# A two-layer graph network on one core: the weight 1 of each node's edge to itself added by GpSimd to the landed stripes, not by a product in every octet of the edge stage

## What is computed

```python
def _gcn_conv(x, W, b, src, dst, ew, n_nodes):
    loop = jnp.arange(n_nodes)
    src2 = concatenate([src, loop]); dst2 = concatenate([dst, loop])
    ew2 = concatenate([ew, jnp.ones((n_nodes,))])
    deg = segment_sum(ew2, dst2)
    dinv = where(deg > 0, rsqrt(maximum(deg, 1e-30)), 0.0)
    norm = dinv[src2] * ew2 * dinv[dst2]
    return segment_sum((x @ W)[src2] * norm[:, None], dst2) + b
```

## Time and profile before

| | us |
|---|---|
| median of 3 runs | 2230.41 |
| lowest and highest | 2229.63, 2230.86 |
| span of the profiled execution (first to last instruction) | 2231.0 |
| busy in the span: PE | 2089.4 (94%) |
| DVE | 1653.8 (74%) |
| ACT | 1233.5 (55%) |
| POOL | 566.9 (25%) |

### The profile page before, as it was taken

The page is one execution under the profiler, slowest core; times in us unless marked ns, Lnnn a source line. Parts: engine busy times, 40 slices in busy tenths (PEclk is TensorE's granted clock), DMA queues, the critical chain, the costliest instruction groups (busy, mean ns, idle before and its releaser), DMA issues. The chain is left out here.

```text
span 2231.0 us, 47270 instructions
## 1 busy us (share of the span) xinstructions
PE 2089.4 (94%) x18287; PEld 1958.7 (88%) x18287; DVE 1653.8 (74%) x3108; ACT 1233.5 (55%) x2876; POOL 566.9 (25%) x406
## 2 busy tenths in 40 slices
PE   5659999999879999998999999999999999999997
PEld 3549999999779999997788999999988999999996
DVE  6899888886578888884667666565667768888885
ACT  5656555555537677674543444444444336767664
POOL 3100000000036777761000000000000015777775
PEclk9879999999989999998999999999999999999998
DMA  4424343333448778775003666466641026777776
GB/s 123 145 65 115 96 114 90 99 111 104 161 158 234 236 218 241 227 222 144 1 26 89 189 188 182 122 182 195 189 145 47 25 93 184 239 231 222 240 215 171
DMA packets 241114, 339.04 MB, mean 152 GB/s; under 512 B 33407, under 2 KB 202546, under 8 KB 240754
## 3 DMA queue, kind: packets, MB, share of 16 engines
q1 hardware_dynamic: 208908, 296.19, 42.4%
q0 software_dynamic: 28528, 35.76, 8.6%
q10 hardware_dynamic: 3446, 3.97, 0.6%
HBM read 258.89 MB, written 76.95 MB: 151 GB/s over the span
## 5 line engine op out<-in xcount | busy, mean ns | idle before, releaser
L2011 POOL DMA_INDIRECT SC<-xd,slot_i x128 | 181.6, 1419 | 1423.8 <-DVE slot_q L1647 1291.6
L2436 PE MATMUL bank<-WB_r,XN_r 128*128 128x448 f32 x1400 | 398.7, 366 | 0.4 <-DVE X L2253 0.4
L2390 DVE TENSOR_TENSOR WB_r<-WB,WB_r 128x448 fp32r<-128x448 f32 x350 | 214.8, 624 | 169.1 <-ACT WB_r L2385 169.0
L2385 ACT CAST WB_r<-WB 128x448 fp32r<-128x448 f32 x350 | 198.2, 568 | 244.8 <-PE bank L2436 242.9
L2436 PEld LDWEIGHTS bank<-WB_r,XN_r 128*128 128x128 f32 x1400 | 262.4, 188 | 23.0 <-DVE X L2253 0.8
L1941 PE MATMUL bank<-SC_r,WB_r 128*128 128x256 f32 (+1 forms) x2064 | 250.8, 280 | 8.4 <-issue 6.3
L1941 PEld LDWEIGHTS bank<-SC_r,WB_r 128*128 128x128 f32 x2064 | 244.3, 188 | 12.6 <-issue 12.4
L1061 ACT CAST WB_r<-bank 128x200 fp32r<-128x200 f32 x391 | 145.3, 372 | 164.7 <-PE bank L1045 163.9
L1956 PE MATMUL bank<-R_r,H_r 128*128 128x256 f32 x1752 | 216.6, 283 | 5.0 <-DVE R_r L1852 5.0
L1956 PEld LDWEIGHTS bank<-R_r,H_r 128*128 128x128 f32 x1752 | 210.4, 190 | 5.4 <-issue 5.4
L1804 ACT ACTIVATE wb_<-bank,WB 128x256 f32<-128x256 f32 (+1 forms) x344 | 133.3, 477 | 79.7 <-PE bank L1941 40.6
(11 more groups left out here) (462 smaller groups left out, 5139.1 us busy)
## 6 DMA issues: line engine op xcount, KB each, us to landing
WB<-adjw SPq DMA_DIRECT2D x350, 224.0 KB, 2.8
WB<-in_f_pack SPq DMA_DIRECT2D x127, 512.0 KB
WB<-in_f_pack SPq DMA_DIRECT2D x62, 640.0 KB
adjw<-X SPq DMA_DIRECT2D x24, 1600.0 KB, 7.6
WB<-in_f_pack SPq DMA_DIRECT2D x65, 516.0 KB
xd<-XN SPq DMA_DIRECT2D x15, 640.0 KB, 5.5
y<-X SPq DMA_DIRECT2D x10, 640.0 KB, 3.3
X<-y SPq DMA_DIRECT2D x6, 640.0 KB, 7.0
```

The costliest lines, as they stand in the source:

```text
L2011: e.indirect_dma_start(yin[i % 2][:, q * D:(q + 1) * D], None, XD, bass.IndirectOffsetOnAxis(ap=slot_i[:, 2 * i + q:2 * i + q + 1], axis=0 ...
L2385: e.copy(split_w(m)[0], RAW[m % PR]).then_inc(S("whigh"), 1)
L2390: e.tensor_tensor(al, RAW[m % PR], ah.bitcast(F32), ALU.subtract).then_inc(S("wlow"), 1)
L2436: mm_ = e.matmul(conv_bank(k, band, c)[:, 0:PW], x[st][:, o], y, start=(st == 0 and i == 0), stop=(st == T - 1 and i == 2))
```

## The change

The product of the identity is gone from every octet; the last of an octet's other products now ends the group and releases ACT. The bf16 copy of the identity goes with it. Instead `own_edges_pool` on GpSimd adds the identity (fp32) to the part of a landed stripe where src is dst, in both convolutions. Such a part is in the stripes that the diagonal crosses: four in each band, 28 in a convolution, 56 in all, of 128 x 128 or 128 x 64 numbers. ACT's rounding of these stripes waits for the addition (semaphore `own`). To have a semaphore for that, three others were merged into two that were there; who waits for whom in them stays as it was.

```diff
-    ident16, iota16 = r1_all[:, 1700:1764].bitcast(BF16), r1_all[:, 1764:1828].bitcast(BF16)
+    iota16 = r1_all[:, 1764:1828].bitcast(BF16)
...
-        c.add(e.tensor_copy(ident16, ident))
...
-        e.tensor_copy(beg4i, beg4).then_inc(S("begins"), 1)
+        e.tensor_copy(beg4i, beg4).then_inc(S("rows"), 1)
...
-        e.wait_ge(S("begins"), 1)
+        e.wait_ge(S("rows"), 2)
...
                 for p in (2, 3):
-                    e.matmul(bk[:, o + KEYS:o + 2 * KEYS], lo, key[:, p * KEYS:(p + 1) * KEYS],
-                             start=False, stop=False, skip_group_check=True)
-            weights = bk[:, 0:8 * KEYS].rearrange("p (q two n) -> p q two n", q=4, two=2)[:, :, 1, 2 * b:2 * b + 2]
-            e.matmul(weights, ident16, ident16[:, 8 * (w % 16):8 * (w % 16) + 8].rearrange("p (q r) -> p q r", q=4),
-                     start=False, stop=True, skip_group_check=True).then_inc(S("win"), 1)
+                    m = e.matmul(bk[:, o + KEYS:o + 2 * KEYS], lo, key[:, p * KEYS:(p + 1) * KEYS],
+                                 start=False, stop=(q == 3 and p == 3), skip_group_check=True)
+            m.then_inc(S("win"), 1)
...
+    def own_columns(n):
+        band, st = divmod(n, T)
+        return max(128 * st, band * PW), min(128 * st + 128, (band + 1) * PW)
...
+    def own_edges_pool(e, k):
+        for n in range(NW):
+            if not has_own(n):
+                continue
+            m = NW * k + n
+            band, st = divmod(n, T)
+            a0, a1 = own_columns(n)
+            block = RAW[m % PR][:, a0 - band * PW:a1 - band * PW]
+            e.wait_ge(S(f"ab{m % PR}"), weights_landed(m))
+            e.tensor_tensor(block, block, ident[:, a0 - 128 * st:a1 - 128 * st], ALU.add).then_inc(S("own"), 1)
+
     def weight_high(e, m):
         e.wait_ge(S(f"ab{m % PR}"), weights_landed(m))
+        if has_own(m % NW):
+            e.wait_ge(S("own"), owns_before(m) + 1)
...
         slots_pool(e, 0, lambda: e.wait_ge(S("y_out"), 80))
+        own_edges_pool(e, 0)
+        own_edges_pool(e, 1)
         between(e, iter(()), lambda i: None, lambda: gather_pool(e, 1, 0), lambda i: None)
```

More of the change, by code:

```diff
@@ L1028, in hots_pe @@
         for w in octets(n):
-            bk, b = B[w % 4], w // 16
+            bk = B[w % 4]
             if w >= 4:
@@ L1330, in degrees_dve @@
             c.wait()
-            e.tensor_scalar(dcol, dcol, 1.0, 1e-30, ALU.add, ALU.max).then_inc(S("degmax"), 1)
+            e.tensor_scalar(dcol, dcol, 1.0, 1e-30, ALU.add, ALU.max).then_inc(S("degroot"), 1)
         if i == 6:
-            e.wait_ge(S("degroot"), 1)
+            e.wait_ge(S("degroot"), 2)
             c.add(e.reciprocal(dcol, dcol))
@@ L1339, in degrees_act @@
         if i == 5:
-            e.wait_ge(S("degmax"), 1)
+            e.wait_ge(S("degroot"), 1)
             e.sqrt(dcol, dcol).then_inc(S("degroot"), 1)
@@ L2379, in conv_sp, with has_own, owns_before @@
             e.dma_start(RAW[m % PR], AW[st * 128:(st + 1) * 128, band * PW:(band + 1) * PW]).then_inc(S(f"ab{m % PR}"), 16)
+    def own_columns(n):
+        band, st = divmod(n, T)
+        return max(128 * st, band * PW), min(128 * st + 128, (band + 1) * PW)
+    def has_own(n):
+        a0, a1 = own_columns(n)
+        return a0 < a1
+    def owns_before(m):
+        return sum(has_own(n % NW) for n in range(m))
+    def own_edges_pool(e, k):
[4 more added lines that the diff above has]
+            band, st = divmod(n, T)
+            a0, a1 = own_columns(n)
+            block = RAW[m % PR][:, a0 - band * PW:a1 - band * PW]
+            e.wait_ge(S(f"ab{m % PR}"), weights_landed(m))
+            e.tensor_tensor(block, block, ident[:, a0 - 128 * st:a1 - 128 * st], ALU.add).then_inc(S("own"), 1)
     def weight_high(e, m):
         e.wait_ge(S(f"ab{m % PR}"), weights_landed(m))
+        if has_own(m % NW):
+            e.wait_ge(S("own"), owns_before(m) + 1)
         if m >= PR:
```

## The result

| | before | changed |
|---|---|---|
| first measurement, median (runs) | 2230.64 (4) | 2219.7 (4) |
| lowest to highest | 2229.63 to 2232.93 | 2217.86 to 2222.83 |
| ratio, 95% interval | | 0.9947 (0.9935 to 0.9958) |
| second measurement, median (runs) | 2221.52 (19) | 2213.78 (5) |
| ratio, 95% interval | | 0.9961 (0.9948 to 0.9974) |

The kernel is faster, as forecast. The first ratio makes 0.0053 x 2230.4 = 11.8 us or 2218.6 us, just under the range's lower end of 2219.5. The two later measurements, on other chips and with more runs of before, both say 0.0039 x 2222 = 8.7 us, where the forecast had 8.8. Chips differ in level by some 10 us (before takes 2221.5 and 2222.5 on two of them, 2230.6 and 2234.3 on others), so only runs of one chip are compared here.

What follows compares the result with a forecast made beforehand. PE was taken to bound the edge stage from 203 to 551 us. Product -8.5, part before 203 -0.3, cast 0, additions 0: -8.8 us from 2230.4, forecast 2221.6 us, range 2219.5 to 2226.

Steps and rivals of the forecast that it cites:

- the range's lower end: Whole kernel: 2220.0 us if all 391 products count, less 0.5 us for scatter, giving 2219.5 us.
- The product's price: Edge stage, 203 to 551 us: each of 335 removed identity products saves 25.5 ns on PE, 8.5 us together.
- The lower bound, nothing gained ahead of fp32 weights: Edge stage after 203: one octet in four saves nothing, leaving a gain of 6.4 us.
- DVE as the next bound: Edge stage after 203: 0.5 us of DVE's 0.6 us room stay, so it doesn't become the bound.
- signs of being wrong: ACT waiting for GpSimd with PE waiting behind; PE idle after 203 in the edge stage; or octets staying at 0.42 us.
- The part before 203: Edge stage's start, where DVE paces or is level: only four PE waits shrink, gaining 0.3 us, 0.4 at most.
- the clock's later rise: Rival, edge stage's start: less PE work delays full clock by some 5 us, costing 2.5 us: 2224 us; chance 0.04.
- The additions: Convolutions: 56 GpSimd additions, taken as 0.6 us each, 1.83 us at most, are covered and cost 0 us.
- The rival that rested on it: Band ends in convolutions: DVE and GpSimd block each other from SBUF, 7 us come back: 2229 us; chance 0.06.
- GpSimd's cover: Convolutions: four additions in a row may last 11.5 us, from landing to PE's use, before PE stops.
- the clock's case: Edge stage's start: full clock comes some 5 us later, priced 2.5 us, time 2224 us; chance 0.04.

Runs made afterwards that it cites:

- e4: Kernel before with the identity's product made twice in every octet: 2231.5 us, ratio to before 1.0032.
- e5: Changed kernel with the identity's product and its bf16 copy put back, additions kept: 2222.38 us, ratio to before 1.0003.
- e9: Changed kernel measured a third time, no edit: 2213.31 us, ratio to before 0.9961.
- e1: Kernel before measured again, no edit: 2233.27 us, ratio 0.9993 to before beside it.
- e6: Changed kernel with 12 products that nobody reads ahead of the second layer's mixing: 2223.43 us, ratio to before 0.9952.
- e3: Changed kernel without the GpSimd additions, so neither product nor additions: 2213.06 us, ratio to before 0.9960.
- e7: Changed kernel with every GpSimd addition made five times, one after the other: 2245.01 us, ratio to before 1.0047.
- e8: Changed kernel with every GpSimd addition made eight times, one after the other: 2342.21 us in one run.
- e2: Changed kernel measured again, no edit: 2213.78 us, ratio to before 0.9961.

## Why the prediction was right and where it was wrong

- **The product's price**: 25.5 ns foreseen, 23.9 measured over 334 octets, 8.0 us instead of 8.5; upward, from e4, 21 ns. The mean hides two prices, 28 ns where PE doesn't wait and less at the ten batches where it does. The lower bound, nothing gained ahead of fp32 weights, didn't come about. The Trainium skill (TensorE: Matmul & The Clock Gate, Back-to-back issue gap) has a floor of about 25 ns for products of up to 64 columns; the runs agree, with 24 to 28 ns. Its formula for a product by itself, 5.8 ns, would have made 1.9 us.
- **DVE as the next bound**: right for most batches, wrong for ten. DVE kept its 283 us of work and its waits fell, and at most batches PE's distance to it shrank as foreseen, from 0.59 to 0.46 us where it repeats. But the prediction read this distance at one batch (357) and called it the smallest that repeats. At ten batches it was 0.07 us already before, so PE waited for DVE there in both kernels, and the change gained 1.3 us less than its 28 ns in every octet would give. PE's idle time after 203 was one of the prediction's own signs of being wrong, and it is there. That the sum came out near all the same is partly luck: a price read 2.3 ns too low stands against stops that were not counted.
- **The part before 203**: 0.7 us lost by batch 28 in the first trace instead of 0.3 us gained, by the clock's later rise. The granted clock went to full for good 28.1 us after the first octet in before's trace and 31.0 us after it in the changed kernel's. Over the thirteen traces with one product or none, batch 28 comes 0.44 us later for each us of that, so the later rise cost 1.3 us; I had it as a rival, at 2.5 us. Whether the change has a part in the rise isn't shown: it lies at 28.1 to 29.6 us in the four traces with one product, and at 28.3 to 29.6 in seven of the nine without, at 30.3 and 31.0 in the other two. Where it lies alike, the product's price here can be read: from the first octet to batch 28 it is 61.8 us in e5 and 61.4 in e9 (rise at 28.6 and 28.7), 62.2 in e1 and 61.8 in e6 (both 29.6). That is 0.4 us for the 0.3 foreseen, and 8.0 + 0.4 = 8.4 us for the product in the whole stage.
- **The additions**: 0 us foreseen, and no more seen (e3, e5; the convolutions last 449.8 us with and without them). Their duration, 0.46 us for 128 columns, was closer to the lower bound than the 0.6 us taken. The Trainium skill (SBUF — State Buffer, Who interferes with whom) lets DVE and GpSimd exclude each other; the trace agrees in so far as DVE's low part takes up to 0.91 instead of 0.62 us beside an addition, and an addition up to 0.95 instead of 0.46. The rival that rested on it needed four times the duration.
- **GpSimd's cover**: 11.5 us foreseen, and e7 puts it at 11.4 (e8 between 9.8 and 11.8). What failed stood in the expectations of e7 and e8: the duration of repeated additions, which left out the waits between them, and the thought that only bands could lose time, where the projection behind the last band and the clock after a stop lose it too.
- **The step that failed** is the range's lower end. To the forecast's own 2220.0 I added 0.5 us "for the scatter of the medians and for the clock's case". The clock's case was there as a loss in one place only. The traces have several places behind waits of PE where a fall of the clock is there in one execution and not in the next, worth 1.5 us in the mixing; in the table's second column the executions differ by another 3.6 us (499.5 to 503.1), in no order that follows the change. Four runs on each side average that badly: the first ratio's interval is some 2.5 us to each side, and the range had 0.5 us for it. The first ratio's 11.8 us hold some 3 us that the edge stage does not have in any trace (8.4 us there) and that two later measurements don't have. That the first measurement's excess over 8.7 us is scatter follows from the table for the profiled pair; for its other runs there is no trace, so for them it is inferred.
- **How much of the scatter is the clock's** differs by chip. In the second measurement before's runs took 2218.9 to 2221.5 us at a mean granted clock of 0.979 (5 runs), 2220.7 to 2223.9 at 0.978 (4), 2221.1 to 2226.3 at 0.977 (7) and 2223.8 to 2226.8 at 0.976 (3), a correlation of -0.79 over 19 runs. In the third it is -0.59 over 21 runs. On e1's chip it is -0.05 over 17 runs, and they still scatter from 2231.3 to 2236.8 us. So the clock is one cause of the scatter and not the only one; what else moves the time there stays open.
- **One rival stays untested**: that the change gains more on chips of the slower level. e6's ratio on such a chip, 0.9952, makes 10.7 us, and its interval doesn't exclude 8.7. In the traces of that chip the edge stage gives the usual 8.4 us (409.2 in e1, 400.9 in e6), and the first octet begins at 143.8 us in e1 and at 140.7 to 141.8 in e6, e7 and e8; with one trace of before there, no run tells whether that is chance.

## What to carry to other kernels

A small matmul in a dense stream costs the distance that it adds from start to start, here 24 ns in the mean and 28 where nothing else stops PE, neither its 166 ns in the list nor its columns; multiply that by the instances in the stretch in which PE waits for nobody. Read the room of the next engine at every batch and not at a typical one: ten of some 170 batches had none here, and the list of waits did not name them before. Before moving work to an idle engine, count the reserve from landing to use, and look at the last piece ahead of a stage that reads the whole result, since no later piece makes up for its delay. And when the expected gain is 0.4%, look first at how much the same kernel differs between two traces, stage by stage.

## What was not expected of the hardware

- The same gap of 1.84 us on PE was followed by 3.4 us at the lower clock in some executions and by none in others (before and e9 against e1, the changed kernel and e2), at a price of 1.5 us each time.
- The same kernel differs by 10 us and more between chips. Most of the difference lies ahead of the edge stage: its first octet begins at 141.4 us in before's trace and at 131 to 133 us in those of the faster chips, while the stages behind it last as long.
- The time at which the clock rose for good at the start of the edge stage differs between executions by up to 2.9 us (28.1 to 31.0 us after the first octet), at 0.44 us for each us.
- A GpSimd `tensor_tensor` of 128 x 128 fp32 numbers takes 0.46 us, one of 128 x 64 0.33 us, and up to 0.95 us beside DVE.
